# Routed tiles of 128 rows in three units, and the last batch's shared FFN issued behind the routed tiles

## What is computed

```python
x = x + layernorm(attention(layernorm(x)))        # q k v, a = q k^T, ctx = a v, group norm, out
h = layernorm(x)
shared = ffn(h, shared_gate, shared_up, shared_down)        # silu(h Wg^T) * (h Wu^T) Wd^T, width 704
topw, topi = top_k(softmax(h @ gate_w.T), 2)                 # 8 experts, two for each token
routed = sum over e of ffn(h, expert e) * weight of e for the token
x = x + layernorm(shared + routed)
```

## Time and profile before

| | us |
|---|---|
| three runs | 981.01, 987.66, 987.77 |
| median | 987.66 |
| the profiled execution | 988.1, with a span of 986.4 on the core |

### The profile page before, as it was taken

One profiled execution on the slowest core, in us unless ns is written; L12 is line 12 of the kernel. 1 busy time (PEld: TensorE's weight loads), 2 busy tenths in 40 slices (PEclk: granted clock), 3 DMA queues, 4 the chain that ended last, 5 costly groups with the idle time before them and its releaser, 6 DMA issues.

```text
span 986.4 us, 22585 instructions
## 1 busy us (share of the span) xinstructions
PE 817.9 (83%) x6598; PEld 674.1 (68%) x6599; DVE 657.5 (67%) x1708; ACT 479.9 (49%) x1065; POOL 307.0 (31%) x342
## 2 busy tenths in 40 slices
PE   4578999899999978474999999999999999999000
PEld 1346767676767656353899988898999888888000
DVE  4689998999898979894455555555555555545065
ACT  2044545455364646241555555555555555555143
POOL 1001000000000000276254444554454555443234
PEclk9789999999999989776999999999999999999655
DMA  4122505041414311301033223223223222332673
GB/s 176 43 96 82 197 23 177 22 176 55 144 59 140 109 68 54 108 11 33 19 54 46 46 43 46 49 51 48 43 43 48 49 47 45 48 43 36 190 234 106
DMA packets 56255, 76.70 MB, mean 78 GB/s; under 512 B 8256, under 2 KB 51008, under 8 KB 55040
## 3 DMA queue, kind: packets, MB, share of 16 engines
q1 hardware_dynamic: 41232, 55.33, 16.4%
q0 software_dynamic: 14976, 20.78, 13.4%
HBM read 48.96 MB, written 27.26 MB: 77 GB/s over the span
## 4 chain that ended last, share of the span: by engine, by line
PE 43%; DVE 24%; DMA 15%; issue 10%; ACT 4%; POOL 2%; POOLq 0%; ACTq 0%; SPq 0%; DVEq 0%
PE ps L780 22%; DMA acc_d<-ysb,idxc 13%; PE ps L795 11%; DVE mx L1078 4%; DVE hf L1052 3%; PE ps L847 3%; PE ps L841 2%; DVE hT L1062 2%; DVE att L1041 2%; DVE att L1204 2%; DVE small L1440 1%; DVE wdn L1111 1%; ACT wdn L756 1%; PE ps L862 1%; PE ps L928 1%
## 5 line engine op out<-in xcount | busy, mean ns | idle before, releaser
L780 PE MATMUL ps<-att,wgu 128*128 128x256 f16 x2574 | 321.7, 274 | 1.9 <-DVE att L1372 1.6
L1052 DVE SCALAR_TENSOR_TENSOR hf<-ps,sc,silu 128x256 f32<-128x256 f32 x330 | 159.4, 483 | 181.9 <-ACT silu L595 158.4
L780 PEld LDWEIGHTS ps<-att,wgu 128*128 x2574 | 252.4, 98 | 34.5 <-issue 4.4
L795 PE MATMUL ps<-wdn,hT 128*128 (+1 forms) x1870 | 259.8, 276 | 13.8 <-DVE hT L1062 11.1
L595 ACT ACTIVATE silu<-ps,sc 128x256 f32<-128x256 f32 x275 | 130.3, 475 | 274.2 <-PE ps L780 273.9
L795 PEld LDWEIGHTS ps<-wdn,hT 128*128 128x128 f16 x1870 | 183.3, 99 | 44.6 <-DVE hT L1062 9.1
L780 PE MATMUL ps<-xhl,wgu 128*128 128x256 f16 x1056 | 138.1, 286 | 6.9 <-DVE hf L1052 6.7
L546 POOL DMA_INDIRECT acc_d<-ysb,idxc x78 | 125.2, 1605 | 57.7 <-POOL idxc L542 31.1
L489 POOL TENSOR_TENSOR rstd<-ve,mhalf 128x4 f32<-128x4 f32 (+1 forms) x32 | 29.8, 931 | 341.8 <-DVE ve L1037 291.9
L780 PEld LDWEIGHTS ps<-xhl,wgu 128*128 128x128 f16 x1056 | 106.9, 103 | 34.3 <-DVE hf L1052 9.9
L1062 DVE TENSOR_TENSOR hT<-hf,hT 128x256 f16<-128x256 f32 x275 | 115.1, 418 | 1.7
(11 more groups left out here) (185 smaller groups left out, 885.1 us busy)
## 6 DMA issues: line engine op xcount, KB each, us to landing
wgu<-in_gu SPq DMA_DIRECT2D x8, 1408.0 KB, 7.5
att<-in_x SPq DMA_DIRECT2D x16, 512.0 KB, 3.8
wdn<-in_dn SPq DMA_DIRECT2D x8, 768.0 KB, 9.7
x_d<-att SPq DMA_DIRECT2D x8, 512.0 KB, 2.9
xn_d<-att SPq DMA_DIRECT2D x8, 512.0 KB, 3.0
acc_d<-ysb SPq DMA_DIRECT2D x16, 256.0 KB, 2.2
wgu<-x_d SPq DMA_DIRECT2D x8, 512.0 KB, 4.6
wdn<-acc_d SPq DMA_DIRECT2D x8, 512.0 KB, 6.0
```

The source lines that it names most:

```text
L780: ins = te.matmul(o, slot_gu(slot, hw, k, j), x(hx, k), start=(n == 0), stop=(n == len(TERMS) - 1))
L795: ins = te.matmul(y_bank(u, tt), h(hh), slot_dn(slot, c, hw), start=(c == 0 and n == 0), stop=(c == FC - 1 and n == 1))
L1052: v.scalar_tensor_tensor(out=hf[lo:P, c % 2 * TW:(c % 2 + 1) * TW], in0=up, scalar=scale_of(slot, 1, lo, P), in1=silu[lo:P, c % 2 * TW:(c ...
```

## The change

Routed tiles have 128 rows and there are 2*4096/128 + 7 = 71 of them. A tile's FFN is done in three units p (`RU`): units 0 and 1 hold two of the old units' blocks of 128 outputs side by side, unit 2 the last one and a half. So a gate and up matmul of the loop has 128 columns of tokens, where it had 256. Rows are gathered four tiles ahead (`XB`), one transfer for a tile, and scattered by one transfer for a tile; the loop's body holds four tiles. The last batch's rows of `acc_d` are set to zero at the start, and its shared FFN, two tiles of six units, moves from `TAIL` to a new table `END` behind the routed loop, where the steps of the final norms stand too: statistics (`c_stats`), root by `pow` on POOL, shift (`c_shift`), addition on POOL (`c_add`) for batches 0 to 6, and for batch 7 `e_rows`, which adds the shared result from PSUM, in two halves. Half of the x2 rows are loaded during the routed loop, to SBUF that is free by then; the loads and stores of batches 0 to 6 give each partition four neighbouring rows. `ORDER`, `LAST_ORDER` and `TAIL` are new orders of their steps, and the attention rotates over four PSUM banks, not three (`NA`), as the shared result needs only one.

```diff
-NTILE = 2 * TOK // TW + E - 1
+NTILE = 2 * TOK // P + E - 1
+RU = 3
+XB = 4
-NA = 3
+NA = 4
...
-TAIL = [("route_top1", 1), ("G", 0), ("G", 1), ("route_top2", 1), ("H", 0), ("route_slots",), ("H", 1), ("route_positions",), ("H", 2),
...
+TAIL = [("route_top1", 1), ("route_top2", 1), ("route_slots",), ("route_positions",), ("one_hots", 0), ("prep_max", 0), ("prep_max", 1),
...
+END = [("H", 0), ("H", 1), ("G", 0), ("H", 2), ("G", 1), ("D", 0), ("H", 3), ("H", 4), ("G", 2), ("G", 3), ("G", 4), ("G", 5), ("G", 6),
...
+         ("H", 8), ("c_stats", 0), ("c_stats", 1), ("c_shift", 0), ("D", 6), ("D", 7), ("c_stats", 2), ("D", 8), ("c_add", 0),
...
             load_stage(0, stg_gu, stg_dn)
+            sp.wait_ge(zero_made, 1)
+            sp.dma_start(acc_d[(B - 1) * S:TOK, :].rearrange("(t p) d -> p t d", p=P),
+                         ysb[:, 0:D].rearrange("p (o d) -> p o d", o=1).to_broadcast([P, NT, D])).then_inc(y_stored, 16)
...
+            for n in range(B):
+                if n == B // 2:
+                    sp.wait_ge(gu_done, QD)
+                sp.dma_start(x2_rows[n], batch_rows(x2_d, n)).then_inc(x2_loaded[n], 16)
+            sp.wait_ge(dn_done, QD)
+            sp.wait_ge(scattered, 16 * NTILE)
+            for n in range(B):
+                sp.dma_start(y_rows[:, n], batch_rows(acc_d, n)).then_inc(acc_loaded[n], 16)
...
+                g.indirect_dma_start(acc_d, bass.IndirectOffsetOnAxis(ap=idxc[:, 4 + r:5 + r], axis=0), ysb[:, r * D:(r + 1) * D], None,
+                                     compute_op=ALU.add).then_inc(scattered, 16)
+                if ahead:
+                    gather_x(i + XB, x, False)
+                pool.wait_ge(scattered, 16 * (i + 1))
...
+            def gate_up_of(i, r, p, slot):
...
+                parts = ((2 * p, 0), (2 * p + 1, P), (5 + 2 * p, TW), (6 + 2 * p, TW + P)) if p < RU - 1 else ((4, 0), (GJ - 1, P), (9, TW))
+                for j, at in parts:
+                    for m, (k, hw, hx) in enumerate(TERMS):
+                        ins = te.matmul(gu_ps[n][:, at:at + P], slot_gu(slot, hw, k, j), xt16[:, r, hx, k, :], start=(m == 0), stop=(m == len(TERMS) - 1))
...
+            def routed(i, x, slot, before, turn=True, later=None):
+                r = x % 2
+                gate_up_of(i, r, 0, slot)
+                if turn:
+                    turn_x(i + 1, (x + 1) % XB, isinstance(i, int) and i == 0)
                 if before is not None:
+                    down_of(i - 1, 1 - r, 1, before)
+                gate_up_of(i, r, 1, slot)
+                if before is not None:
+                    down_of(i - 1, 1 - r, 2, before)
                 after = later() if later else None
+                gate_up_of(i, r, 2, slot)
+                down_of(i, r, 0, slot)
```

More of the change, by code:

```diff
@@ new lines, in _, with cmb_root @@
+            for i in range((NTILE - XB) // XB * XB, NTILE):
+                scatter(i, i % XB, i + XB < NTILE)
+            def cmb_root(m, cols):
+                pool.wait_ge(cmb_ve, m + 1)
+                if m >= 4:
+                    pool.wait_ge(cmb_norm, m - 3)
+                g.tensor_tensor(rstd[m % 4][:, 0:cols], ve[m % 4][:, 0:cols], mhalf[:, 0:cols], ALU.pow).then_inc(cmb_rstd, 1)
+            for step in END:
+                if step[0] == "c_stats":
+                    cmb_root(step[1], NT)
+                if step[0] == "e_rows":
+                    cmb_root(B - 1 + step[1], TT)
+                if step[0] == "c_add":
+                    n = step[1]
+                    pool.wait_ge(x2_loaded[n], 16)
+                    pool.wait_ge(cmb_norm, n + 1)
+                    g.tensor_tensor(x2_rows[n], x2_rows[n], y_rows[:, n], ALU.add).then_inc(out_made, 1)
@@ new lines, in tile_out, with routed @@
+            def tile_out(i, r):
+                act.wait_ge(dn_done, QR + RU * (i + 1))
+                wait(act, y_added, i)
+                act.wait_ge(yw_made, i + 1)
+                passed(act)
+                a.activation(ysb[:, r * D:(r + 1) * D], y_ps[r][:, 0:D], ACT.Copy, scale=yw[:, r:r + 1]).then_inc(y_made, 1)
+            def routed(i, r, slot, first=False, turn=True):
+                if not first:
+                    high_of(i - 1, 1 - r, 2)
+                silu_of(i, r, 0, slot)
@@ L751, in scaling @@
-            def scaling(g, r):
-                act.wait_ge(cmb_nmr, GB * g + r + 1)
-                passed(act)
-                rows = rows_of(y_rows, g, r)
-                for t in range(NT):
-                    a.activation(rows[:, t, :], rows[:, t, :], ACT.Identity, bias=cmb_shift[r][:, t:t + 1],
-                                 scale=rstd[r][:, t:t + 1]).then_inc(cmb_norm, 1)
-            with act.Fori(0, NGRP) as g:
-                for r in range(GB):
-                    deviation(g, r)
-                    scaling(g, r)
+            routed(NTILE - 1, 0, s2, turn=False)
@@ new lines, in cmb_scale @@
+            def cmb_scale(m, rows):
+                act.wait_ge(cmb_nmr, m + 1)
+                for t, row in enumerate(rows):
+                    ins = a.activation(row, row, ACT.Identity, bias=cmb_shift[m % 4][:, t:t + 1], scale=rstd[m % 4][:, t:t + 1])
+                ins.then_inc(cmb_norm, 1)
+            for step in END:
+                kind = step[0]
+                if kind == "H" and step[1] == 0:
+                    high_of(NTILE - 1, 0, 2)
+                if kind in "GDH":
+                    ffn_step(kind, step[1], SH, 0)
+                if kind == "H" and step[1] == 1:
+                    tile_out(NTILE - 1, 0)
+                if kind == "c_shift":
+                    cmb_scale(step[1], [y_rows[:, step[1], t, :] for t in range(NT)])
+                if kind == "e_shift":
+                    cmb_scale(B - 1 + step[1], [y_rows[:, B - 1, TT * step[1] + t, :] for t in range(TT)])
@@ new lines, in down_of @@
+            def down_of(i, r, p, slot):
+                q = QR + RU * i + p
+                if p == 0:
+                    pe.wait_ge(y_made, SH * TT if isinstance(i, int) and i == 0 else SH * TT - 1 + i)
+                pe.wait_ge(lo_made, q + 1)
+                for cc in range(2):
+                    c = 2 * p + cc
+                    pairs = ((0, 0), (0, 1), (1, 0)) if c < FC - 1 else ((0, 0), (0, 1))
+                    for m, (hh, hw) in enumerate(pairs):
+                        at = (2 * p + hh) * TW + cc * P
+                        ins = te.matmul(y_ps[r][:, 0:D], hT[:, at:at + P], slot_dn(slot, c, hw), start=(c == 0 and m == 0), stop=(c == FC - 1 and m == 1))
+                ins.then_inc(dn_done, 1)
@@ L954, in routed @@
-                down(t, r, 2, slot)
+                gate_up_of(i, r, 2, slot)
+                down_of(i, r, 0, slot)
                 return after
```

531 lines of the change are left out of this document (268 added, 263 removed), and 24 rows, old and new, of tables (LAST_ORDER, ORDER, TAIL).

## The result

| | before | after |
|---|---|---|
| median of the runs, us | 986.73 | 1137.55 (1135.08 to 1141.27) |
| ratio to before | | 1.155, 95% interval 1.151 to 1.159 |
| profiled execution, us (span) | 988.1 (986.4) | 1141.3 (1139.5) |

The change makes the kernel 15.5% slower. The forecast was 1147 us, with a range of 1085 to 1215.

A forecast was written before the change was run, and what follows sets the result against it. PE's full array bounds the routed loop before; after, its sequencer's address instructions would. From 988 us: tail -12, loop +195, end -23, batches -1 gives 1147 us, range 1085 to 1215.

The forecast's parts named there:

- The loop: Routed loop: PE's sequencer sets the pace at 9.0 us a tile, 71 tiles 639 us in place of 444.7, +195.
- the reading of the number: Routed loop, PE's sequencer: loading the expert's number into a register takes 0.7 us a tile.
- The cover: Routed loop: sequencer work of 9.6 us at most hid behind 11.35 of matmuls; now 9.0 stand against 5.7.
- Rival 1: Routed loop: address instructions do not bind, array and handoffs give 5.9 us a tile, 926 us in all; chance 0.08.
- rival 2: Routed loop: cheaper steps or extras, or dearer short matmuls; 7 to 8.4 us a tile, 1055 us (1005 to 1105); chance 0.10.
- Rival 3: Routed loop: PE's clock falls, with a mix at some 10.1 us a tile and 1225 us in all; chance 0.10.
- The tail and the batches: Ahead of the loop: tail -12 (-6 to -16) as DVE loses work; batches -1 (-8 to +8), DVE still binding.
- POOL's 48 halves stay and lie beside DVE: Tail: POOL's one-hot halves, 29 us, run beside DVE's work while 10.8 us leave DVE.
- The end: Behind the loop: shallower pipeline, one scatter, earlier x2 loads, then POOL as chain; about 52 us, -23 (-12 to -30).
- worth nothing while that wait and the norms last: End: the moved shared FFN, 21.8 us of matmuls, is hidden; 5 to 10 us if PE runs at the low clock.
- most ended by no other engine (issue): Routed loop, expected sign: most of PE's gaps end without another engine releasing them.
- PE busy about 60%: Routed loop, expected sign: PE's busy share, from 5.7 of 9.0 us a tile, with granted clock 0.9 or more.

## Why the prediction was right, step by step

**The loop, +195 forecast, +187.6 measured.** The mechanism is shown from both sides: without addresses the loop falls to 6.04 us a tile (forecast for the array and handoffs 5.9), a fifth fewer addresses take off their share, more matmuls cost nothing, and the kernel before does not feel them. The sum was 9.0 us a tile, the transposes give 8.87. Its terms: the steps at 0.128 (mean 0.128 by their starts, 0.118 by removal), the reading of the number at 0.7 (0.68 by removal), and the rest, which 8.87 - 56 x 0.128 - 0.68 leaves at 1.0 where I had 1.1.

**The cover.** "Before, the sequencer's work for a tile hid behind 11.35" is confirmed by 444.7 us with and without it.

**Rivals.** Rival 1 (the addresses do not bind, 926) describes the kernel without addresses, 937, and not the changed one. The 81 ns a matmul under rival 2 fell with the 56 ns of that run. Rival 3 did not come: the granted clock in the loop is 1.00, though the array could do a tile in 6.04 of 8.87 us. I had compared with the tail, where the matmuls come in short groups with gaps of us between; here the gaps lie between single matmuls, which is what I had named against it.

**The tail and the batches, -13 forecast, -16.1 measured.** The sum is near, but its parts are not, and they make up for one another. By the row of the split of x, 1.0 us is gained ahead of the first split, 9.8 up to the last one and 5.3 from there to the loop. So the tail's -12 was too much and the batches' -1 too little. In the tail the step that failed is "POOL's 48 halves stay and lie beside DVE". The gain is all in the inversions, 35.5 us from the first to the last where there were 41.1 (415.1 to 456.2 before, 404.6 to 440.1 now). With the FFN gone DVE waits for POOL there: taking a third of POOL's one-hot halves away, in the kernel with wide tiles, shortened the inversions by 5.3 us. I had that as the lower bound, -6. In the batches I held DVE to be full at 42.19 of 45.00 and so gave the new order and the fourth bank nothing. But 45.00 was one of the shorter batches: five in the middle take 228.3, 45.7 each, and now 44.4. The other gain, some 6 us between the splits of batches 6 and 7, goes at least by half with the new `LAST_ORDER`, for which I had no term. Executions also differ: with the first transposes of the kernels that are the same up to the loop at 444.1 to 448.4, and those of before at 461.7 and 463.7, the gain ahead of the loop is 13 to 20 us.

**The end, -23 forecast, -18.4 measured.** The failed step is "worth nothing while that wait and the norms last" for the shared FFN: it costs 6.4 us. I had priced it on PE only, 200 matmuls beside a wait, with 5 to 10 us if PE ran at the low clock. The size came within that, but not for that reason: the granted clock was 1.00 until 1098.70, and only the few matmuls behind that ran at the lower level (six down matmuls take 1.46 us from 1110.39, where six take 0.82 at 1098.56). Its price is 1.8 us in the chain from PE to DVE ahead of the first statistics, and 4.6 behind them, where two low halves stand between the shifts of the norms and are held up by POOL's additions. The rows of the accumulator came when I said, 16 us behind the loop (first statistics at 15.8 without the FFN); with it the first statistics start at 17.7 (1100.25). Without the FFN the end takes 50.4 us (1079.2 to 1129.6), where my terms, 16, 25.4 and 8 to 10, add up to 50 or 51 and I wrote 52. The root on POOL, for which I had no row and took 1.0, takes 1.01.

**What I said the profile would show.** The tile period, the steps and the clock came as written. Gaps "most ended by no other engine (issue)" did not, since the view puts 34.6 of 39.0 us of them down to DVE's product, wrongly as it turned out. Nor did "POOL's additions back to back": the seven start 4.1 us apart on average (1107.24 to 1131.62), and the eight of before 4.9. The tail at 44 did not come either, with 5.3 us gained where 12 were forecast. "PE busy about 60%" was wrong too: the row says 576.27 of 632.30, 91%. A matmul's record is 219 to 228 ns long while they start 85 ns apart, so the records overlap, and gaps of 30 ns between the matmuls close in the sum. The share of busy time could not have told the two cases apart; without addresses it is 98% (412.53 of 422.60) at a tile of 6.04.

## What to carry to other kernels

When a tile is made smaller, count what does not shrink with it. Here that was one register instruction for each weight block, 56 a tile, at 0.12 us a step: hidden as long as the matmuls behind each lasted longer, and the bound as soon as they were halved. Before cutting a tile whose addresses come from registers, multiply the sequencer's instructions by their step (from start to start, not by the length that the profile shows) and compare with the array's time for the tile. And when work is moved into a stretch where one engine waits, price it on all the engines that it uses, since the others may be the chain there.

## What the runs showed of the hardware

- An address instruction is shown as 46 ns and takes the sequencer 0.12 to 0.13 us, whether one matmul or up to three stand behind it (8.87 and 8.89 us a tile).
- PE's busy share says little on short matmuls: 91% and 98% for loops of which one has a third of the array's time free.
- The releaser of a wait can be an engine that had nothing to do with it. 0.6 us a tile put down to DVE's product were PE's own reading of a number into a register.
- Some small DVE instructions stretch to about the end of POOL's addition of 128x1024 beside them, as a low half did with 2.46 us for 0.41; the statistics beside such an addition kept their 1.40 us for four.
